# Top-2 experts on one Trainium2 core: inner rows made turned, from weights picked by VectorE, with the bias inside the gelu

## The reference

```python
logits = xf @ gate_w + gate_b
probs = jax.nn.softmax(logits, axis=-1)
top2_vals, top2_idx = jax.lax.top_k(probs, 2)
# for each expert e, with weight cw[:, e] that is 0 where e was not chosen:
h = jax.nn.gelu(xf @ W1[e] + b1[e], approximate=False)   # 256 -> 512
y = h @ W2[e] + b2[e]                                    # 512 -> 256
out += cw[:, e][:, None] * y
```

## Time and profile before

| What | us |
|---|---|
| median of three runs | 8055.03 (8054.05 to 8055.25) |
| span of the profiled execution | 9107.5 |
| first expert phase, first transpose to last scatter issue | 3918.1 to 4357.0 |
| second expert phase, the same | 8597.6 to 9036.0 |

### The profile page before, as it was taken

The page is one execution under the profiler, slowest core; times in us unless marked ns, Lnnn a source line. Parts: engine busy times, 40 slices in busy tenths (PEclk is TensorE's granted clock), DMA queues, the critical chain, the costliest instruction groups (busy, mean ns, idle before and its releaser), DMA issues. The chain is left out here.

```text
span 9107.5 us, 91729 instructions
## 1 busy us (share of the span) xinstructions
PE 5351.0 (59%) x20514; PEld 4012.4 (44%) x20515; DVE 3669.3 (40%) x8808; ACT 3376.1 (37%) x8020; POOL 4734.0 (52%) x4927
## 2 busy tenths in 40 slices
PE   3789555555534444789433335456556466566796
PEld 2656333444423333656433333344445344445564
DVE  7544555555710000544300001455455455455644
ACT  2522233333333333445333333233334233333553
POOL 5113455555466666034366664666564666664143
PEclk8689776777767776789555555677677767777698
DMA  1421333333233333211201111333332333332213
GB/s 56 178 74 61 91 92 91 86 88 91 67 94 92 92 91 92 84 54 63 79 22 23 23 23 32 94 88 92 87 91 71 95 93 91 88 88 77 94 63 124
DMA packets 395135, 723.41 MB, mean 79 GB/s; under 512 B 117204, under 2 KB 252470, under 8 KB 391602
## 3 DMA queue, kind: packets, MB, share of 16 engines
q0 software_dynamic: 210544, 509.17, 20.1%
q1 hardware_dynamic: 177622, 201.65, 6.9%
q10 hardware_dynamic: 6508, 8.01, 0.2%
HBM read 600.76 MB, written 123.53 MB: 80 GB/s over the span
## 5 line engine op out<-in xcount | busy, mean ns | idle before, releaser
L952 POOL DMA_INDIRECT g_rows<-table,src_idx x2352 | 2244.2, 954 | 1407.4 <-issue 669.9
L1227 PE MATMUL g_p_win<-g_rows,g_hot 128*128 128x264 f32 (+1 forms) x4704 | 1555.7, 490 | 42.5 <-issue 36.0
L1227 PEld LDWEIGHTS g_p_win<-g_rows,g_hot 128*128 128x128 f32 x4704 | 1105.9, 246 | 309.8 <-issue 72.3
L1117 ACT ACTIVATE g_hot<-iota,near 128x128 f32<-128x128 f32 x2352 | 721.4, 387 | 1199.0 <-DMA r_gb<-in_L_ffn_gate_b_dram 873.0
L952 POOL DMA_INDIRECT g2p_rows<-rows,src_idx x784 | 749.3, 956 | 370.4 <-issue 227.7
L952 POOL DMA_INDIRECT gcnp_rows<-table,src_idx x784 | 748.2, 954 | 368.6 <-issue 228.8
L1033 DVE TENSOR_TENSOR g_rows<-g_rows,g_p_w 128x1792 f32<-128x1792 f32 x336 | 679.0, 2021 | 51.1 <-issue 21.2
L1241 PE MATMUL g_p_f<-ones 1*128 1x4 f32 (+1 forms) x336 | 85.9, 324 | 863.9 <-issue 414.1
L1189 PE MATMUL gcnp_p_out<-gcnp_win,gcnp_moved 128*128 128x64 f32 x224 | 62.0, 432 | 732.4 <-ACT gcnp_win L1151 629.7
L1040 DVE TENSOR_TENSOR agg<-agg,g2p_p_out 128x256 f32 x112 | 42.1, 418 | 1102.6 <-PE g2p_p_out L1189 454.1
L1241 PEld LDWEIGHTS g_p_f<-ones 1*128 1x128 f32 x336 | 72.0, 265 | 931.5 <-issue 931.5
(11 more groups left out here) (832 smaller groups left out, 11533.3 us busy)
## 6 DMA issues: line engine op xcount, KB each, us to landing
g_rows<-table,src_idx POOLq DMA_INDIRECT x2352
back<-agg SPq DMA_DIRECT2D x7, 1792.0 KB, 35.0
g_inj<-inject SPq DMA_DIRECT2D x56, 224.0 KB
g2p_rows<-rows,src_idx POOLq DMA_INDIRECT x784
rows<-r_row SPq DMA_DIRECT2D x98, 128.0 KB
gcn_row_in<-back SPq DMA_DIRECT2D x14, 896.0 KB
gcnp_rows<-table,src_idx POOLq DMA_INDIRECT x784
c_row<-back SPq DMA_DIRECT2D x14, 896.0 KB, 13.3
```

Of the source, the lines that this page charges most:

```text
L952: gp.indirect_dma_start(rows[:, s, j, 0:width + H], None, table, bass.IndirectOffsetOnAxis(g.src_idx[:, at:at + 1], 0)).then_inc(got[s], 16)
L1117: last = nc.scalar.activation(hot[:, j, :], g.iota[:, :], ACT.Square, scale=-1.0, bias=g.near[:, bass.ds(c * J + j, 1)])
L1227: last = nc.tensor.matmul(p_win[:, 0:W], hot[:, j, :], rows[:, s, j, :], start=(j == 0), stop=(j == J - 1))
```

## The change

The product with W1 is turned around. The stationary operand is now a 128x128 block of W1 and the moving operand the 128 turned rows, so `p_h` comes out with the hidden features on the partitions and needs no transpose. For that:

- PE: `first` makes four blocks of 128 hidden features, two matmuls of 128 columns for each (L2896 of the new kernel); `turn_hidden` is gone, `second` reads what ACT wrote and moves one step forward (lead 0, was -1).
- DVE: `bias` and `copy_hidden` are gone. A new `pick` (lead 2) copies the expert's whole W1, 128x1024, from `w1s` into one of two buffers `w1c`; `first` reads it there, at an address fixed in the program.
- ACT: `curve` takes the gelu straight from `p_h` into `ht`, in four instructions of 128x128, with b1 as a bias for each partition. Its loop body now has four tiles and loads expert numbers too. `copy` stays.
- b1 is loaded once as 32 rows of 128 (`b1r`), transposed by PE and copied by DVE at the phase's start; the eight spread loads of `b1s` are gone.

```diff
     def load(self, eng, placed):
         F = self.F
+        eng.dma_start(self.b1r[:, :], self.b1.rearrange("e (b p) -> (e b) p", p=P)).then_inc(self.b_in, 16)
         for e in range(E):
...
-            eng.dma_start(self.b1s[:, e, :], self.b1[one, :].to_broadcast([P, F])).then_inc(self.w_in, 16)
...
-        hb, hg, ht = ph.sb("hb", [P, 2, F]), ph.sb("hg", [P, 2, F]), ph.sb("ht", [P, 2, HB, P])
+        ht, b1t = ph.sb("ht", [P, 2, HB, P]), ph.sb("b1t", [P, E, HB])
+        w1c = ph.sb("w1c", [P, 2, 2 * F])
...
-        p_h = [ph.ps(f"p_h{s}", [P, F]) for s in range(2)]
-        p_t = [ph.ps(f"p_t{s}", [P, HB, P]) for s in range(2)]
+        p_h = [ph.ps(f"p_h{s}", [P, HB, P]) for s in range(2)]
+        p_b = ph.ps("p_b", [P, E * HB])
...
             @block.tensor
             def _(pe):
-                for s in (turned, up, h_turned, down):
+                pe.wait_ge(wt.b_in, 16)
+                nc.tensor.transpose(p_b[:, :], wt.b1r[:, :], g.ident[0:E * HB, 0:E * HB]).then_inc(b_turned, 1)
+                for s in (turned, up, down):
...
                 def first(i, s, at):
                     pe.wait_ge(copied, i + 3)
-                    pe.wait_ge(biased, i + 1)
-                    for k in range(2):
-                        last = nc.tensor.matmul(p_h[s % 2][:, :], xt[:, s % 2, k, :], w1s[:, of(at), k * F:(k + 1) * F].rearrange("p a f -> p (a f)"), start=(k == 0), stop=(k == 1))
+                    pe.wait_ge(picked, i + 1)
+                    pe.wait_ge(curved, i + 1)
+                    for b in range(HB):
+                        for k in range(2):
+                            last = nc.tensor.matmul(p_h[s % 2][:, b, :], w1c[:, s % 2, k * F + b * P:k * F + (b + 1) * P], xt[:, s % 2, k, :], start=(k == 0), stop=(k == 1))
                     last.then_inc(up, 1)
 
-                def turn_hidden(i, s, at):
+                def second(i, s, at):
                     pe.wait_ge(curved, i + 3)
-                    pe.wait_ge(h_copied, i + 1)
-                    for b in range(HB):
-                        last = nc.tensor.transpose(p_t[s % 2][:, b, :], hg[:, s % 2, b * P:(b + 1) * P], g.ident[:, :])
-                    last.then_inc(h_turned, 1)
-
-                def second(i, s, at):
-                    pe.wait_ge(h_copied, i + 3)
                     pe.wait_ge(made, i + 1)
...
-                pipeline(pe, TILES, [(2, turn), (1, first), (0, turn_hidden), (-1, second)], AHEAD, before=before)
+                pe.wait_ge(w_in, 32 * E)
+                pipeline(pe, TILES, [(2, turn), (1, first), (0, second)], AHEAD, before=before)
...
                 def curve(i, s, at):
-                    ac.wait_ge(biased, i + 3)
-                    ac.wait_ge(h_turned, i + 1)
-                    nc.scalar.activation(hg[:, s, :], hb[:, s, :], ACT.Gelu).then_inc(curved, 1)
-                pipeline(ac, TILES, [(2, copy), (1, curve)])
+                    ac.wait_ge(up, i + 3)
+                    ac.wait_ge(down, i + 1)
+                    for b in range(HB):
+                        last = nc.scalar.activation(ht[:, s % 2, b, :], p_h[s % 2][:, b, :], ACT.Gelu, bias=b1t[:, of(at), b:b + 1].rearrange("p a f -> p (a f)"))
+                    last.then_inc(curved, 1)
+                before, of = experts(ac, ACTE)
+                ac.wait_ge(b_ready, 1)
+                pipeline(ac, TILES, [(2, copy), (1, curve)], AHEAD, before=before)
...
-                def bias(i, s, at):
-                    dv.wait_ge(up, i + 3)
-                    dv.wait_ge(curved, i + 1)
-                    nc.vector.tensor_tensor(hb[:, s % 2, :], p_h[s % 2][:, :], b1s[:, of(at), :].rearrange("p a f -> p (a f)"), ALU.add).then_inc(biased, 1)
+                def pick(i, s, at):
+                    dv.wait_ge(up, i + 1)
+                    nc.vector.tensor_copy(w1c[:, s % 2, :], w1s[:, of(at), :].rearrange("p a f -> p (a f)")).then_inc(picked, 1)
...
-                def copy_hidden(i, s, at):
-                    dv.wait_ge(h_turned, i + 3)
-                    dv.wait_ge(down, i + 1)
-                    nc.vector.tensor_copy(ht[:, s % 2, :, :], p_t[s % 2][:, :, :]).then_inc(h_copied, 1)
-
-                pipeline(dv, TILES, [(1, bias), (0, copy_hidden), (-1, out)], AHEAD, peeled=AHEAD, before=before)
+                pipeline(dv, TILES, [(2, pick), (0, out)], AHEAD, peeled=AHEAD, before=before)
```

More of the change, by code:

```diff
@@ L2556, in __init__ @@
         self.w1s = spare[:, 0:E * 2 * F].rearrange("p (e k f) -> p e (k f)", e=E, k=2)
-        self.b1s = spare[:, E * 2 * F:E * 3 * F].rearrange("p (e f) -> p e f", e=E)
-        self.w2s = sb("w2s", [P, E, self.HB * D])
-        self.w_in = nc.alloc_semaphore(f"{name}_w_in")
+        self.w2s, self.b1r = sb("w2s", [P, E, self.HB * D]), sb("b1r", [E * self.HB, P])
+        self.w_in, self.b_in = nc.alloc_semaphore(f"{name}_w_in"), nc.alloc_semaphore(f"{name}_b_in")
     def load(self, eng, placed):
         F = self.F
+        eng.dma_start(self.b1r[:, :], self.b1.rearrange("e (b p) -> (e b) p", p=P)).then_inc(self.b_in, 16)
         for e in range(E):
@@ L2822, in experts_by_tile @@
     F, HB = wt.F, wt.HB
-    w1s, b1s, w2s, w_in = wt.w1s, wt.b1s, wt.w2s, wt.w_in
+    w1s, w2s, w_in = wt.w1s, wt.w2s, wt.w_in
     with Phase(nc, name) as ph:
-        ph.sems.append(w_in)
+        ph.sems += [w_in, wt.b_in]
         b2s, b2_in = ph.sb("b2s", [P, E, D]), ph.sem("b2_in")
@@ L2828, in experts_by_tile @@
         xt = ph.sb("xt", [P, 2, 2, P])
-        hb, hg, ht = ph.sb("hb", [P, 2, F]), ph.sb("hg", [P, 2, F]), ph.sb("ht", [P, 2, HB, P])
+        ht, b1t = ph.sb("ht", [P, 2, HB, P]), ph.sb("b1t", [P, E, HB])
+        w1c = ph.sb("w1c", [P, 2, 2 * F])
         y = ph.sb("y", [P, AHEAD, D])
         p_x = [ph.ps(f"p_x{s}", [P, 2, P]) for s in range(2)]
-        p_h = [ph.ps(f"p_h{s}", [P, F]) for s in range(2)]
-        p_t = [ph.ps(f"p_t{s}", [P, HB, P]) for s in range(2)]
+        p_h = [ph.ps(f"p_h{s}", [P, HB, P]) for s in range(2)]
+        p_b = ph.ps("p_b", [P, E * HB])
         p_y = [ph.ps(f"p_y{s}", [P, D]) for s in range(2)]
-        turned, copied, up, biased, curved, h_turned, h_copied, down, made = (
-            ph.sem(n) for n in ("turned", "copied", "up", "biased", "curved", "h_turned", "h_copied", "down", "made"))
+        b_turned, b_ready, picked, turned, copied, up, curved, down, made = (
+            ph.sem(n) for n in ("b_turned", "b_ready", "picked", "turned", "copied", "up", "curved", "down", "made"))
         x_in = [ph.sem(f"x_in{s}") for s in range(AHEAD)]
@@ L2846, in before @@
                 eng.nop(nofuse=True)
-                loaded[:] = registers(nc, engine, g.tile_expert[0:1, bass.ds(t + AHEAD - 1, steps + 2)], E - 1, waited=False)
-            return before, lambda place: bass.ds(loaded[place + 1], 1)
+                loaded[:] = registers(nc, engine, g.tile_expert[0:1, bass.ds(t + AHEAD, steps + 2)], E - 1, waited=False)
+            return before, lambda place: bass.ds(loaded[place], 1)
         with nc.Block() as block:
@@ L2907, in second @@
                     last.then_inc(down, 1)
-                pe.wait_ge(w_in, 48 * E)
-                pipeline(pe, TILES, [(2, turn), (1, first), (0, turn_hidden), (-1, second)], AHEAD, before=before)
+                pe.wait_ge(w_in, 32 * E)
+                pipeline(pe, TILES, [(2, turn), (1, first), (0, second)], AHEAD, before=before)
             @block.scalar
@@ L2918, in copy @@
                     ac.wait_ge(up, i + 1)
-                    nc.scalar.activation(xt[:, s, :, :], p_x[s][:, :, :], ACT.Identity).then_inc(copied, 1)
+                    nc.scalar.activation(xt[:, s % 2, :, :], p_x[s % 2][:, :, :], ACT.Identity).then_inc(copied, 1)
                 def curve(i, s, at):
-                    ac.wait_ge(biased, i + 3)
-                    ac.wait_ge(h_turned, i + 1)
-                    nc.scalar.activation(hg[:, s, :], hb[:, s, :], ACT.Gelu).then_inc(curved, 1)
-                pipeline(ac, TILES, [(2, copy), (1, curve)])
+                    ac.wait_ge(up, i + 3)
[6 more added lines that the diff above has]
+                pipeline(ac, TILES, [(2, copy), (1, curve)], AHEAD, before=before)
             @block.vector
             def _(dv):
-                for s in (biased, h_copied, made):
-                    nc.vector.sem_inc(s, 2)
-                dv.wait_ge(w_in, 48 * E)
+                nc.vector.sem_inc(made, 2)
+                dv.wait_ge(b_turned, 1)
+                nc.vector.tensor_copy(b1t[:, :, :].rearrange("p e b -> p (e b)"), p_b[:, :]).then_inc(b_ready, 1)
+                dv.wait_ge(w_in, 32 * E)
                 dv.wait_ge(b2_in, 16)
                 before, of = experts(dv, DVE)
-                def bias(i, s, at):
-                    dv.wait_ge(up, i + 3)
-                    dv.wait_ge(curved, i + 1)
-                    nc.vector.tensor_tensor(hb[:, s % 2, :], p_h[s % 2][:, :], b1s[:, of(at), :].rearrange("p a f -> p (a f)"), ALU.add).then_inc(biased, 1)
+                def pick(i, s, at):
```

(2 more changed lines are left out.)

## The result

The changed kernel takes 7974.41 us (median of four runs, 7969.26 to 7978.20), the kernel before 8054.54 us beside it (8053.87 to 8055.25): a ratio of 0.990 with an interval of 0.9886 to 0.9914, 80.1 us less. The forecast was 7974, a gain of 81.

The account below looks back on a forecast made before the run. PE was taken to bound both expert phases; 79 us from shorter tiles plus 2 from the filling made 81, so 8055 - 81 = 7974 us, with a range of 7958 to 8005.

Parts of the forecast that it names:

- What bounds: Both expert phases: PE is the bound, busy for 432 of 434 us, with nothing else near it.
- The tile: PE's tile in the expert phases: 4.10 us becomes 3.72, 0.38 less, 79 us over 2 x 105 tiles.
- The rival of unhidden loads: `first`: sixteen weight loads not hidden, 4.85 us, run at 8622; chance 0.05 together with a lower clock.
- The filling: Start of each expert phase: pipeline one stage shorter, 1 us gained a phase, 2 in all.
- ACT's loaded tile: Tile with both table loads: gelus end at S + 4.9 to 5.1, needed at S + 5.7; slack 0.6 to 0.8, cost zero.
- The expert numbers: ACT's load of expert numbers in the tile with both table loads: 0.28 us, in before the turn is done.
- `pick`: DVE's copy of W1 at the head of a body: 0.7 us, slack 0.7 to 1.4, cost zero.
- The front: Eight b1 loads leave each front, hidden behind a DVE chain: 0 taken, up to 4 us gained in both.
- The gap of 1052 us: Profiled span against median of runs: PE's gapless expert phases lose nothing without the profiler, so 81 us carry over whole, not 72.
- A late hand-over: ACT's loaded tile or `pick` misses its slack, PE waits once in four tiles: 8000 to 8026; chance 0.06.
- The double table switch: ACT loses another 1.28 us behind each table load, PE waits 1.8 us a body: 8068; chance 0.03.
- the lighter front: Fronts: taking spread b1 out may give nothing, which was already the value taken; no chance of its own.

Follow-up runs that it names:

- transposes: Changed kernel with four transposes of a constant per tile put back on PE ahead of `second`, read by nobody: 8064.38 us, ratio 1.0012 to the kernel before.
- act_two: Changed kernel with ACT's loop body at two tiles instead of four, so its table loads double: 7974.96 us, ratio 0.9904 to the kernel before.
- before_act_four: Kernel before with only ACT's loop body made four tiles, which halves its table loads: 8053.78 us, ratio 0.9999.
- dear_pick: Changed kernel with `pick` written as the maximum of W1 with itself, two operands instead of one: 7974.19 us, ratio 0.9903 to the kernel before.
- third_set: Changed kernel with a one-column square root on ACT in each four-tile body, needing one more table load: 8034.02 us, ratio 0.9975 to the kernel before.
- spread_b1: Changed kernel with the eight spread loads of b1 put back into the front, read by nobody: 7974.96 us, ratio 0.9902 to the kernel before.
- b_again: Kernel before, unchanged, run once more for a second profile: 8059.53 us in a single run, with a span of 8057.7.

## Why the prediction was right, step by step

- **What bounds.** PE alone, before and after: 393.67 of 394 us busy, and 0.44 us more work on it cost 90 us (transposes), while 133 us more or less on ACT (act_two, before_act_four) and 112 us more on DVE (dear_pick, 210 x 0.53) cost or gave nothing.
- **The tile.** 3.72 forecast, 3.733 measured. A pair of `first` costs 1.79 / 16 = 0.112 us, against 0.1114 from the earlier trace rows; its weight load lasts 192 ns by its own row and is hidden, as there. Over 85 tiles in a row the two traces have 4.103 and 3.734 us a tile, so the gain in the tiles is 0.369 x 210 = 77.5 us, 1.5 less than forecast. The rival of unhidden loads, with 4.85 us for `first`, is out. The rule of the Trainium skill that it stood on ("TensorE: Matmul & The Clock Gate", "The mechanism": a load overlaps matmuls in flight only where the row groups differ) doesn't hold for these 3360 pairs. The same section also lets a load into the background weight buffer be pulled ahead, which the prediction passed over; which buffer these loads used, no run here shows.
- **The filling.** A phase has 396.2 - 105 x 3.734 = 4.1 us of it, where it had 436.6 - 105 x 4.103 = 5.8: 1.7 less each, 3.4 in both, against 2 forecast. The first `second` starts 8.1 us after the first `turn` (12.2 before), which are the 4 us that the prediction named; more of them counted than it took. The two misses cancel, and that the forecast came within 1 us of the measured time is luck to that extent: 77.5 + 3.4 = 80.9 against 80.1 in the runs, whose own spread is 9 us.
- **ACT's loaded tile.** The end was right, S + 5.13 against S + 4.9 to 5.1, and so was its deadline, S + 5.74 against 5.7 (S = 3547.51, the start of `turn`). The way there was not. *The expert numbers* were put at 0.28 us "in before the turn is done"; they take 1.40 (here 1.38, from S - 0.55 to S + 0.83), and the first table load starts at S + 1.0, not S + 0.5. The copy then ends at S + 2.67, not S + 2.2, and the second load starts 0.4 late; four gelus in 1.14 us instead of 1.25 won 0.1 back. The hand-over to PE, 0.24 us, was left out altogether. So the slack is 0.40 by third_set, below the stated 0.6 to 0.8: the cost of zero was right by a smaller margin than was claimed. The price was taken from ACT's load in the graph phase, which loads *one* number (`at, = info(ACTE, c, 3, 1)` in the kernel); a body of four tiles loads six. The row of DVE's load of the same six numbers, 0.81, was nearer, though still short.
- **`pick`.** 683 ns forecast as 0.7; slack 1.45 against 0.7 to 1.4. The one-operand row was the right choice, and the other end, 1.44, would have cost nothing either: dear_pick shows it up to 1.22 us, and the slack covers the rest.
- **The front.** Zero, as taken (spread_b1, 128.4 against 128.2 us).
- **The gap of 1052 us.** 950 us of it lay between the gathers of the graph phases (b_again), so the unscaled 81 was right. The prediction argued it from PE's rows in the expert phases; where the excess lay it couldn't say with one profile.
- **The rivals.** A late hand-over didn't come; third_set shows its price, 52 us for each us of wait in a body, as computed, and that 0.4 us more on ACT would have brought it. Its chance of 0.06 was low for that margin. The double table switch is refuted by the rows of third_set. That the lighter front gives nothing was the value taken, and it came so.

## What to carry to other kernels

Where one engine is busy for 99% of a stretch, price an edit by the distance between starts on that engine alone, and look for the same instruction form elsewhere in the trace before believing that smaller pieces are dearer: 0.1114 us from another phase held to 1%. For every other engine compute the slack at its worst tile, the one that carries the loop's own cost (register loads, table loads), not its mean share: ACT, busy for 57% of the phase, had 0.4 us left. A load of loop numbers into registers belongs in that sum, priced from a row that loads as many numbers, on the same engine where there is one. So does the hand-over to the engine that waits, here 0.24 us.

## What the runs showed of the hardware

- **Register loads.** The same load of six expert numbers takes 0.81 us on DVE and 1.40 on ACT. The time grows with the count: ACT's load of a single number takes 277 ns (PE's loads in the kernel before take 301 ns for one number and 818 for six). With bodies of two tiles (act_two), where four numbers are loaded, ACT's takes 1127 ns by its line below. Why ACT needs longer than DVE for the same six is open, and so is why its median is 1386 ns in the changed kernel's first expert phase and 1563 in its second.

```profile
L92 ACTq TENSOR_LOAD <-tile_expert x11: 1111/1127/1159, 3522.3 to 3596.9; - x11
```

- **POOL beside DVE.** A scatter's issue that *starts* while DVE runs `pick`, with 0.3 us or more of it left, lasts until some 0.88 us after `pick` ends: in dear_pick one that starts with 0.33 us of `pick` left takes 1.21 us, and one with 1.10 left 1.98 (the rows at 3551.05 and 3853.51), against 1.02. One that starts ahead of `pick` isn't held: 1.01 us at 3554.78, although `pick` began at 3555.05. In the changed kernel, with its one-operand copy, only 12 of the 210 scatters start inside `pick`; they take 1.26 to 1.45 us, and those that start 0.27 ahead of it 1.08. So the copy's two-operand form is not needed for the effect. This fits the "GPSIMD Engine Reference" of the Trainium skill, section "Specifications", by which POOL shares SBUF interfaces with DVE and collides with its instructions of two SBUF inputs or in a two-port mode; whether the one-operand copy runs in such a mode, no run here shows. It costs nothing here: POOL has room, and `y` and `xin` have four buffers each (not two, as the section on the kernel before says of all tiles).
- **One execution's gathers.** Between the same 2352 indirect gathers, one execution idled 690 us more than another, with the gathers no longer (b_again).
